# Linear attention and an fp8 product on one core: V's product moved ahead of the inter product, the fp8 and output products behind the intra product, and the output read one step later

## The chip, the cores and the metric

The kernel runs on one core of a Trainium2 chip. A core has TensorE (matmuls), VectorE, ScalarE and GpSimd (elementwise work and reductions) and SyncE, whose queue here starts most of the DMAs. Each engine executes its own instructions in program order and waits on semaphores for the others. The metric is device time in microseconds (us), lower is better; the kernel before takes 1250.56 us (median of 3 runs, 1250.27 to 1251.45).

## The reference, cut to what matters

```python
xn = layernorm(x)                                # x: (4, 2048, 512)
q, k, v = (heads(xn @ W.T + b) for W, b in ...)  # 64 heads of 8
q, k = softmax(be * q), softmax(be * k)          # over the 8 values of a head, be = exp(beta)
kv = cumsum(einsum('zsD,zsd->zsDd', k, v), axis=1)
kn = cumsum(k, axis=1)
att = einsum('zsD,zsDd->zsd', q, kv) / sum(q * kn, axis=-1)
ffn = fp8(clip(xn / s_in, -448, 448)) * s_in @ (w_fp8 * s_w).T + bias
out = x + (att @ Wo.T + bo) + ffn                # att with its heads joined again
```

## The kernel before, in words

The sequence is cut into 64 steps of 32 positions; with four sequences a tile has 128 rows, and a step handles one such tile of x (128 x 512). Prefix sums are done in chunks: within a step, scores of q and k are masked to the lower triangle and multiplied with v (the "intra product", L1018); what came before the step is in a running state, and q times this state is the "inter product" (L999). Both add up in the PSUM tile `a_ps`, in which the step's own state update (k times v, `state()`, L917) stands before; VectorE must have read that (`mask_state`, L654) before L999 may overwrite it.

Products of fp32 accuracy are made from pairs of fp16 matmuls. Projecting K, Q or V (`project()`, L873 to L877) is 12 matmuls of 128x128x512, the output product (`project_out()`, L884 to L888) 12 more, and the fp8 product (L975) 4. V's projection, the fp8 product and the output product use the same PSUM tile `vo_ps`. For step i it is filled in turn by: V's projection of i; VectorE's `scale_values(i)` (L727) reads it and writes `vp`; ScalarE copies the output bias into it (the seed, L477, signalled by `oseed_ready`); the fp8 product and then the output product of step i-2 add to it; VectorE's `output()` (L720) reads it, adds the residual and writes `o_sb`.

The four compute engines each have a function `body(i)`, and it alone sets the order on its engine. The engines are joined by counting semaphores. In program order one `body(i)` issues, with t = i-1:

- TensorE: K(i); scores of t, first half, and state update; transposes of the normalised attention of i-2; Q(i); scores and state, second half; fp8(i-2); output product(i-2); inter product(t); V(i); intra product(t).
- VectorE: normalise attention(i-2) (L682, L690); xn(i+1) (L618); fp8 clip (L637); row maximum and shift of K (L643, L647), which needs K(i); two masks of scores (L671); first `mask_state`; low part of the attention (L748); key sums and the transpose of k (L699 to L711); maximum and shift of Q; fp8 rounding constants (L624, L629); two masks; the transpose `qT` (L769), which needs ScalarE's exponential of Q; second `mask_state`; `output(i-2)`; `add_state` (L665); statistics of x; `scale_values(i)`.
- ScalarE: the seed for step i-2; copies of xn; exponential of K; seed of K; high part of the attention; `k_pairs`; exponential of Q; seed of Q; `q_heads(i)`, four masked copies of `qT` (L521); `st_seqs`, four masked copies of the running state (L530).
- SyncE's queue: moves of `vp` into `v_groups` (8 DMAs, step i-1); turned copies of x; loads of x; the store of out(i-2); the load of the residual.

Steps 0 to 3 and 60 on are written out; between them the compute engines other than TensorE loop over groups of four steps. TensorE has all steps written out for weights whose low fp16 part is zero in the fp8 product, as here.

Of the kernel before, what the change touches and what calls it, by code (L numbers as in the profile page):

```python
# [28 lines left out]
ACT = mybir.ActivationFunctionType  # L29
# [3 lines left out]
SEQS = 4  # L33
TOK = P // SEQS
# [4 lines left out]
J = 4  # L39
GP = 2  # L40
SP = 2
# [81 lines left out]
def build(nc, x, wq, bq, wk, bk, wv, bv, wo, bo, beta, wf, bf, in_scale, w_scale, const, out):  # L123
# [3 lines left out]
    with ExitStack() as ctx:  # L127
# [173 lines left out]
        def _(sp):  # L301
# [29 lines left out]
            def body(i):  # L331
                if (i - 1).exists():
                    move_v(i - 1)
                if (i + 1).exists():
                    turn_x(i + 1)
                if i.exists():
                    turn_xq(i)
                if (i + SLOTS).exists():
                    load_x(i + SLOTS)
                t = i - 2  # L340
                if t.exists():
                    sp.wait_ge(o_ready, (t + 1).n)
                    sp.dma_start(out_t[t.n], o_sb[:, t.parity, :]).then_inc(stored[t.parity], 16)
                if i.exists():
                    sp.dma_start(x_res[:, i.parity, :], x_t[i.n]).then_inc(r_loaded[i.parity], 16)
# [14 lines left out]
            for i in range(STEPS + 2):  # L360
                body(Step(0, i))
# [89 lines left out]
        def _(act):  # L451
# [16 lines left out]
            def body(i, last_weights=None, fold=False):  # L468
                t = i - 2
                if t.exists():  # L470
                    if (t + 1).exists():
                        act.wait_ge(vp_ready, (t + 2).n)
                    else:
                        act.wait_ge(o_ready, t.n)
                    if t.off == 0 and isinstance(t.k, int):
                        act.wait_ge(fold_ready, 1)
                    sc.activation(vo_ps[:, :], bias[:, 3, :], ACT.Copy, scale=out_up[:, :])\  # L477
                        .then_inc(oseed_ready, 1)
# [22 lines left out]
                if i.exists():  # L501
# [21 lines left out]
                    last.then_inc(qheads_ready, 1)  # L523
                t = i - 1
# [51 lines left out]
        def _(dve):  # L576
# [154 lines left out]
            def body(i, last_weights=None, fold=False):  # L731
# [5 lines left out]
                if i.exists():  # L737
                    if i.after(1):
                        quantise(i)
                    shift(i, k_ps, k_done, k_max, kmax_ready, k_shift, kshift_ready, ke_ready)  # L740
# [121 lines left out]
        def _(pe):  # L862
# [58 lines left out]
            def body(i, low_part=True, last_weights=None, fold=False):  # L921
# [42 lines left out]
                if fold:  # L964
# [4 lines left out]
                    project_out(rest=False).then_inc(bvo_done, 1)  # L969
                t = i - 2  # L970
# [15 lines left out]
                t = i - 1  # L986
                if t.exists():
                    pe.wait_ge(qT_ready, (t + 1).n)
                    if i.exists():
                        pe.wait_ge(masked_ready, (t + 1).n * 2)  # L990
                    else:
                        pe.wait_ge(an_ready, t.n)
                    if t.after(1):
                        pe.wait_ge(stseqs_ready, t.n)
                    for n in range(2):
                        for gp in range(GP):
                            for u in range(J):
                                g = G // 2 * n + GP * u + gp
                                mm(a_rows[TOK * u:TOK * (u + 1), n, gp, :], qT[:, t.parity, g, :],  # L999
                                   st_seqs[:, t.parity, g].rearrange("p j b w -> p (j b w)"),  # L1000
                                   start=(gp == 0), stop=False, skip_group_check=True)
                if i.exists():
                    if fold:
                        pe.wait_ge(fold_ready, 1)
                    if (i - 2).exists():
                        pe.wait_ge(o_ready, (i - 1).n)
                    project(vo_ps, i, MV, seeded=False).then_inc(v_done, 1)
                if t.exists():
                    pe.wait_ge(att_ready, (t + 1).n * 4)
                    for b in range(SEQS):  # L1010
                        pe.wait_ge(v_moved[t.parity][b], (t + 2).half * 16 * GP)
                    pe.sem_inc(pe_waited, 1)
                    for h in range(2):
                        for n in range(SEQS // SP):
                            for j in range(J):
                                cols = slice(GW * j + SP * VW * n, GW * j + SP * VW * (n + 1))
                                for u in range(J):
                                    last = mm(a_rows[TOK * u:TOK * (u + 1), h, :, cols],  # L1018
                                              att[:, n, J * h + u, j, :],
                                              v_groups[:, t.parity, :, n, J * h + u, j, :], start=False, stop=True,  # L1020
                                              skip_group_check=True)
                    last.then_inc(a_done, 1)
# [71 lines left out]
```

## Time and profile before

| | kernel before |
|---|---|
| median of 3 runs | 1250.56 us |
| profiled execution | 1250.03 us |
| its span, first to last instruction | 1248.2 us |
| mean granted TensorE clock over the span | 0.982 of full |
| TensorE matmuls, busy | 1174.9 us (94%) |
| VectorE, busy | 977.9 us (78%) |
| ScalarE, busy | 744.9 us (60%) |
| GpSimd, busy | 321.6 us (26%) |
| DMA, mean of the core | 84 GB/s |

The profiled execution stands beside the runs: 1250.03 against 1250.56 us. A page of the profile gives shares over the whole span; the question of a change in order is answered by views in time order, where each row is an instruction (or a run of equal ones) with its start, its length and, in brackets, the idle time of its engine before it and who ended it. Matmuls are pipelined: a row's length of 0.38 us holds the pipeline's depth, and what a matmul costs in a dense run is the distance to the next start, 0.22 us.

### The profile page before, as it was taken

The page shows a single profiled execution, that of the slowest core. Times are in us where ns is not written, and L with a number is a line of the kernel's source. Part 1 is how long each engine was busy: PE and PEld are TensorE (multiplying, and loading weights), DVE is VectorE, ACT ScalarE, POOL GpSimd, SP SyncE. Part 2 cuts the span into 40 slices and gives each one's busy share as a digit, 9 for nine tenths or more (in the row PEclk, how much of TensorE's full clock was granted, in tenths as well). Part 3 has the DMA queues.
Part 4 walks back from the last instruction along what each step waited for, and adds up shares of the span by engine and source line. Part 5 has one row for each costly group of instructions (what it writes and reads, how often), then busy time and mean ns, then how long its engine had stood idle before and what let it go on. Part 6 is the DMA issues. An engine that isn't in the chain of part 4 may idle for free.

```text
span 1248.2 us, 60447 instructions
## 1 busy us (share of the span) xinstructions
PE 1174.9 (94%) x26082; PEld 679.2 (54%) x26082; DVE 977.9 (78%) x1968; ACT 744.9 (60%) x1177; POOL 321.6 (26%) x590
## 2 busy tenths in 40 slices
PE   1459999999999999999999999999999999999996
PEld 1235555555555555555555555555555555555553
DVE  4567887888788788878878887788788778878873
ACT  0456656665666666566666656666665666566652
POOL 3122222322222232222223232222323232222310
PEclk9689999999999999999999999999999999999999
DMA  9022334334334433433333343343343433333331
GB/s 234 21 59 70 81 90 89 78 80 91 82 82 87 89 80 79 90 86 80 85 89 82 77 90 89 78 84 91 81 79 91 84 83 81 91 82 81 72 73 46
DMA packets 156483, 104.64 MB, mean 84 GB/s; under 512 B 111968, under 2 KB 128480, under 8 KB 156256
## 3 DMA queue, kind: packets, MB, share of 16 engines
q1 hardware_dynamic: 155536, 99.76, 35.7%
q8 instruction: 209, 3.42, 1.2%
q10 hardware_dynamic: 720, 1.31, 0.4%
q14 instruction: 18, 0.15, 0.0%
HBM read 40.20 MB, written 16.78 MB: 46 GB/s over the span
## 4 chain that ended last, share of the span: by engine, by line
PE 92%; issue 3%; DVE 2%; DMA 1%; ACT 1%; POOL 1%; SPq 0%; POOLq 0%; DVEq 0%; ACTq 0%
PE s_ps L900 10%; PE a_ps L917 7%; PE a_ps L1018 6%; PE a_ps L999 6%; PE k_ps L873 5%; PE vo_ps L975 5%; PE vo_ps L873 5%; PE k_ps L877 5%; PE k_ps L875 5%; PE vo_ps L884 4%; PE vo_ps L888 4%; PE vo_ps L886 4%; PE vo_ps L877 4%; PE vo_ps L875 4%; PE q_ps L877 4%; PE q_ps L873 4%
## 5 line engine op out<-in xcount | busy, mean ns | idle before, releaser
L521 ACT ACTIVATE q_heads<-qT,cst 128x512 f32<-128x512 f32 x256 | 163.9, 711 | 88.2 <-DVE qT L769 88.2
L407 POOL TENSOR_TENSOR y_sum<-y,y_magic 128x512 f32<-128x512 f32 x64 | 81.4, 1272 | 433.0 <-DVE y_magic L629 433.0
L506 ACT ACTIVATE w_own<-kT,cst 128x512 f32<-128x512 f32 x128 | 85.5, 715 | 166.7 <-DVE kT L711 166.7
L530 ACT ACTIVATE st_seqs<-st_run,cst 128x576 f32<-128x576 f32 x252 | 181.5, 797 | 0.5 <-DVE st_run L665 0.5
L671 DVE TENSOR_TENSOR att<-s_ps,cst 128x512 f32<-128x512 f32 x256 | 163.8, 682 | 0.4 <-PE s_ps L900 0.4
L400 POOL TENSOR_TENSOR x_split<-xn,x_split 128x512 f16<-128x512 f32 x64 | 74.1, 1158 | 291.6 <-ACT x_split L462 284.3
L900 PE MATMUL s_ps<-q_heads,w_own 64*64 64x128 f32 x4096 | 141.3, 275 | 0.6 <-DVE att L671 0.6
L900 PEld LDWEIGHTS s_ps<-q_heads,w_own 64*64 64x64 f32 x4096 | 110.4, 132 | 54.3 <-issue 54.2
L462 ACT ACTIVATE x_split<-xn 128x512 f16<-128x512 f32 x64 | 40.3, 630 | 126.7 <-DVE xn L618 126.7
L873 PE MATMUL k_ps<-w_hi,xT 128*128 128x512 f16 x256 | 98.9, 386 | 17.0 <-DMA xT<-x_split 12.3
L727 DVE TENSOR_TENSOR vp<-vo_ps,vp 128x512 f32<-128x512 f32 x64 | 44.3, 692 | 86.3 <-PE vo_ps L877 86.3
L884 PE MATMUL vo_ps<-w_hi,ah 128*128 128x512 f16 x260 | 98.5, 379 | 0.6 <-DVE al L748 0.6
L888 PE MATMUL vo_ps<-w_hi,al 128*128 128x512 f16 x260 | 98.5, 379 | 0.0
L886 PE MATMUL vo_ps<-w_lo,ah 128*128 128x512 f16 x260 | 98.5, 379 | 0.0
L875 PE MATMUL k_ps<-w_lo,xT 128*128 128x512 f16 x256 | 98.3, 384 | 0.0
L877 PE MATMUL k_ps<-w_hi,xT 128*128 128x512 f16 x256 | 98.3, 384 | 0.0
L873 PE MATMUL vo_ps<-w_hi,xT 128*128 128x512 f16 x256 | 97.7, 382 | 0.0
L917 PE MATMUL a_ps<-vp,k_e 32*32 32x36 f32 x8064 | 97.6, 196 | 0.0
L873 PE MATMUL q_ps<-w_hi,xT 128*128 128x512 f16 x256 | 97.0, 379 | 0.0
L875 PE MATMUL q_ps<-w_lo,xT 128*128 128x512 f16 x256 | 97.0, 379 | 0.0
L877 PE MATMUL q_ps<-w_hi,xT 128*128 128x512 f16 x256 | 97.0, 379 | 0.0
L875 PE MATMUL vo_ps<-w_lo,xT 128*128 128x512 f16 x256 | 97.0, 379 | 0.0
(136 smaller groups left out, 2287.8 us busy)
## 6 DMA issues: line engine op xcount, KB each, us to landing
v_groups<-vp SPq DMA_DIRECT2D x512, 36.0 KB, 3.1
x_in<-L_attn_x SPq DMA_DIRECT2D x64, 256.0 KB
x_res<-L_attn_x SPq DMA_DIRECT2D x64, 256.0 KB
out<-o_sb SPq DMA_DIRECT2D x64, 256.0 KB
w_own<-L_attn_Wk SPq DMA_DIRECT2D x1, 1024.0 KB, 13.0
w_own<-L_attn_Wq SPq DMA_DIRECT2D x1, 1024.0 KB, 15.0
w_own<-L_attn_Wv SPq DMA_DIRECT2D x1, 1024.0 KB, 16.5
att<-L_ffn_weight_fp SPq DMA_DIRECT2D x1, 1024.0 KB, 18.1
```

The costliest lines, as they stand in the source:

```text
L506: last = sc.activation(k_pairs[:, i.parity, :, c, :], kT[:, :, :], ACT.Copy, scale=pair_mask[:, c:c + 1])
L521: last = sc.activation(q_heads[:, i.parity, :, j, :], qT[:, i.parity, :, :], ACT.Copy, scale=head_mask[:, j:j + 1])
L530: last = sc.activation(st_seqs[:, i.parity, :, :, b, :].rearrange("p g j w -> p (g j) w"), st_run[:, :, :, :].rearrange("p g j w -> p (g j ...
L671: v.tensor_tensor(att[:, c % 2, 4 * (c // 2):4 * (c // 2) + 4, :, :] .rearrange("p g j s -> p (g j) s"), s_ps[:, DM * (c % 2):DM * (c % 2 ...
L873: mm(bank[:, :], xT[:, t.parity, 0, c, :], w_hi[:, m, c, :], start=(c == 0 and not seeded), stop=False, skip_group_check=seeded)
L875: mm(bank[:, :], xT[:, t.parity, 0, c, :], w_lo[:, m, c, :], start=False, stop=False, skip_group_check=seeded)
L877: last = mm(bank[:, :], xT[:, t.parity, 1, c, :], w_hi[:, m, c, :], start=False, stop=(c == KC - 1), skip_group_check=seeded)
L884: mm(vo_ps[:, :], ah[:, j, :], w_hi[:, MO, j, :], start=(j == 0 and not rest), stop=False, skip_group_check=rest)
L886: mm(vo_ps[:, :], ah[:, j, :], w_lo[:, MO, j, :], start=False, stop=False, skip_group_check=rest)
L888: last = mm(vo_ps[:, :], al[:, j, :], w_hi[:, MO, j, :], start=False, stop=(j == J - 1), skip_group_check=rest)
L900: last = mm(s_ps[SP * TOK * gp:SP * TOK * (gp + 1), DM * n + P * q:DM * n + P * (q + 1)], k_pairs[rows, t.parity, g, :, :].rearrange("p c ...
L917: last = mm(a_ps[rows, col:col + J * VW], k_e[rows, t.parity, TOK * g:TOK * (g + 1)], vp[rows, t.parity, v_head(g):v_head(g) + J, :], star ...
```

## The change

On TensorE, `body(i)` ends in another order: V(i), inter product(t), intra product(t), fp8(i-2), output product(i-2), where before it was fp8, output, inter, V, intra. ScalarE's seed for i-2 moves from the start of `body(i+1)` to `body(i)`, behind `q_heads(i)` and ahead of `st_seqs`. VectorE's `output()` moves from behind the second `mask_state` of `body(i)` to the next body, ahead of K's maximum; `scale_values(i)` comes directly behind `add_state`, and the statistics behind it. On SyncE's queue the moves of v(i) stand last in the body, and the store goes one step later. No instruction is added or removed. With two lines more in the file, line numbers differ: L999 becomes L991, L1018 becomes L1004, L975 becomes L1014, L477 becomes L522, L769 becomes L771.

The end of a step on TensorE before, from the last three matmuls of the output product on (`ah`, `al`: attention, high and low part; `st_seqs`: the running state):

```order
L884 MATMUL vo_ps<-w_hi,ah 128x512
L886 MATMUL vo_ps<-w_lo,ah 128x512
L888 MATMUL vo_ps<-w_hi,al 128x512
L999 MATMUL a_ps<-st_seqs,qT 32x144 [waits stseqs_ready,masked_ready,qT_ready]
L999 MATMUL a_ps<-st_seqs,qT 32x144 x15
L873 MATMUL vo_ps<-w_hi,xT 128x512 [waits o_ready]
L875 MATMUL vo_ps<-w_lo,xT 128x512
L877 MATMUL vo_ps<-w_hi,xT 128x512
```

And now the same place, from the last of V's matmuls on:

```order
L877 MATMUL vo_ps<-w_lo,xT 128x512
L879 MATMUL vo_ps<-w_hi,xT 128x512
L991 MATMUL a_ps<-st_seqs,qT 32x144 [waits stseqs_ready,masked_ready,qT_ready]
L991 MATMUL a_ps<-st_seqs,qT 32x144 x15
L1004 MATMUL a_ps<-v_groups,att 32x2x18 [waits v_moved0_2,v_moved0_3,v_moved0_1,att_ready,v_moved0_0]
L1004 MATMUL a_ps<-v_groups,att 32x2x18 x63
L1014 MATMUL vo_ps<-w_hi,xq 128x512 [waits oseed_ready,xq_turned]
L1014 MATMUL vo_ps<-w_hi,xq 128x512 x3
L886 MATMUL vo_ps<-w_hi,ah 128x512 [waits al_ready,ah_ready]
```

V's projection is what now stands between the second state update and the inter product, where the fp8 and the output product stood; the inter and the intra product are neighbours, and they alone stand between V and the fp8 product, which waits on `oseed_ready`.

ScalarE in the same step, before:

```order
L512 ACTIVATE q_e<-q_shift,q_exp_scale 128x512 [waits qT_ready,qshift_ready]
L515 ACTIVATE q_ps<-bias 128x512
L521 ACTIVATE q_heads<-qT,cst 128x16x32 [waits scores_done,qT_ready]
L521 ACTIVATE q_heads<-qT,cst 128x16x32 x3
L530 ACTIVATE st_seqs<-st_run,cst 128x64x9 [waits a_done,strun_ready]
L530 ACTIVATE st_seqs<-st_run,cst 128x64x9 x3
L477 ACTIVATE vo_ps<-bias,out_up 128x512 [waits vp_ready]
L459 REGISTER_ALU
```

ScalarE now:

```order
L502 ACTIVATE q_e<-q_shift,q_exp_scale 128x512 [waits qT_ready,qshift_ready]
L505 ACTIVATE q_ps<-bias 128x512
L511 ACTIVATE q_heads<-qT,cst 128x16x32 [waits scores_done,qT_ready]
L511 ACTIVATE q_heads<-qT,cst 128x16x32 x3
L522 ACTIVATE vo_ps<-bias,out_up 128x512 [waits vp_ready]
L530 ACTIVATE st_seqs<-st_run,cst 128x64x9 [waits a_done,strun_ready]
L530 ACTIVATE st_seqs<-st_run,cst 128x64x9 x3
L459 REGISTER_ALU
```

The seed (`vo_ps<-bias,out_up`) has gone ahead of the four `st_seqs` copies, and still stands behind the four `q_heads` copies.

VectorE from the second pair of score masks on, before:

```order
L671 TENSOR_TENSOR att<-s_ps,cst 128x512 [waits scores_done] x2
L769 STREAM_TRANSPOSE qT<-q_e 128x512 [waits a_done,qheads_ready,qe_ready]
L654 TENSOR_TENSOR st_masked<-a_ps,cst 128x288 [waits state_done]
L720 SCALAR_TENSOR_TENSOR o_sb<-vo_ps,out_dn,x_res 128x512 [waits stored0,r_loaded0,o_done]
L662 REGISTER_ALU
L665 TENSOR_TENSOR st_run<-st_run,st_masked 128x576 [waits stseqs_ready,masked_ready]
L592 BN_STATS stats<-x_in 128x6 [waits x_loaded1]
```

VectorE now:

```order
L671 TENSOR_TENSOR att<-s_ps,cst 128x512 [waits scores_done] x2
L771 STREAM_TRANSPOSE qT<-q_e 128x512 [waits a_done,qheads_ready,qe_ready]
L654 TENSOR_TENSOR st_masked<-a_ps,cst 128x288 [waits state_done]
L662 REGISTER_ALU
L665 TENSOR_TENSOR st_run<-st_run,st_masked 128x576 [waits stseqs_ready,masked_ready]
L727 TENSOR_TENSOR vp<-vo_ps,vp 128x64x8 [waits krec_ready,v_done]
L592 BN_STATS stats<-x_in 128x6 [waits x_loaded1]
```

The read of the output has left this place; what stands ahead of the second `mask_state` (L654) is unchanged.

The diff, without the parts that only repeat moved lines:

```diff
@@ SyncE, body(i)
-                if (i - 1).exists():
-                    move_v(i - 1)
                 if (i + 1).exists():
                     turn_x(i + 1)
                 if i.exists():
                     turn_xq(i)
                 if (i + SLOTS).exists():
                     load_x(i + SLOTS)
-                t = i - 2
+                t = i - 3
                 if t.exists():
                     sp.wait_ge(o_ready, (t + 1).n)
                     sp.dma_start(out_t[t.n], o_sb[:, t.parity, :]).then_inc(stored[t.parity], 16)
+                if (i - 1).exists():
+                    sp.dma_start(x_res[:, (i - 1).parity, :], x_t[(i - 1).n]).then_inc(r_loaded[(i - 1).parity], 16)
                 if i.exists():
-                    sp.dma_start(x_res[:, i.parity, :], x_t[i.n]).then_inc(r_loaded[i.parity], 16)
+                    move_v(i)
@@ ScalarE, body(i): taken from its start, put behind q_heads
+                t = i - 2
+                if t.exists():
+                    if i.exists():
+                        act.wait_ge(vp_ready, (i + 1).n)
+                    else:
+                        act.wait_ge(o_ready, t.n)
+                    if t.off == 0 and isinstance(t.k, int):
+                        act.wait_ge(fold_ready, 1)
+                    sc.activation(vo_ps[:, :], bias[:, 3, :], ACT.Copy, scale=out_up[:, :])\
+                        .then_inc(oseed_ready, 1)
@@ VectorE, body(i)
                     if i.after(1):
                         quantise(i)
+                    if (i - 3).exists():
+                        output(i - 3)
                     shift(i, k_ps, k_done, k_max, kmax_ready, k_shift, kshift_ready, ke_ready)
...
-                if (i - 2).exists():
-                    output(i - 2)
                 if t.exists() and i.exists():
                     add_state(t)
+                if i.exists():
+                    scale_values(i)
                 if (i + 3).exists():
                     statistics(i + 3)
                 if i.parity == 0 and (i + PAIR).exists():
                     variances(i + PAIR)
-                if i.exists():
-                    scale_values(i)
+                if not (i + 1).exists() and (i - 2).exists():
+                    output(i - 2)
@@ TensorE, body(i): V, taken from behind the inter product
+                if i.exists():
+                    if fold:
+                        pe.wait_ge(fold_ready, 1)
+                    if (i - 3).exists():
+                        pe.wait_ge(o_ready, (i - 2).n)
+                    project(vo_ps, i, MV, seeded=False).then_inc(v_done, 1)
                 t = i - 1
                 if t.exists():
                     pe.wait_ge(qT_ready, (t + 1).n)
...
                     last.then_inc(a_done, 1)
+                t = i - 2
+                if t.exists():
+                    pe.wait_ge(xq_turned, (t + 1).n * 16)
+                    pe.wait_ge(oseed_ready, (t + 1).n)
...
+                    last.then_inc(f_done, 1)
+                t = i - 2
+                if t.exists():
+                    pe.wait_ge(ah_ready, (t + 1).n)
+                    pe.wait_ge(al_ready, (t + 1).n)
+                    project_out(rest=True).then_inc(o_done, 1)
```

## Rows read from the trace of the kernel before

**Rows 1.** The page: busy shares, and TensorE's busy share and clock in 40 slices.

```profile
PE 1174.9 (94%) x26082; PEld 679.2 (54%) x26082; DVE 977.9 (78%) x1968; ACT 744.9 (60%) x1177; POOL 321.6 (26%) x590
...
PE   1459999999999999999999999999999999999996
...
PEclk9689999999999999999999999999999999999999
```

**Rows 2.** The chain that ended last, by engine (page, part 4).

```profile
PE 92%; issue 3%; DVE 2%; DMA 1%; ACT 1%; POOL 1%; SPq 0%; POOLq 0%; DVEq 0%; ACTq 0%
```

**Rows 3.** TensorE in time order: start us, us, engine, line, shapes, count, [idle before].

```profile
616.96 0.84 PE L917 MATMUL a_ps<-vp,k_e 32*32 32x36 f32 x64
617.73 1.04 PE L975 MATMUL vo_ps<-w_hi,xq 128*128 128x512 f16 x4
...
620.98 0.38 PE L888 MATMUL vo_ps<-w_hi,al 128*128 128x512 f16 x1
621.53 1.19 PE L999 MATMUL a_ps<-st_seqs,qT 128*32 128x144 f32 x32 [0.17 <-issue]
622.65 0.39 PE L873 MATMUL vo_ps<-w_hi,xT 128*128 128x512 f16 x1
...
625.34 1.32 PE L1018 MATMUL a_ps<-v_groups,att 128*32 128x36 f32 x128
626.60 0.39 PE L873 MATMUL k_ps<-w_hi,xT 128*128 128x512 f16 x1
...
628.98 0.38 PE L877 MATMUL k_ps<-w_hi,xT 128*128 128x512 f16 x1
```

**Rows 4.** VectorE in time order, same columns: an even step.

```profile
611.13 0.69 DVE L643 TENSOR_REDUCE k_max<-k_ps 128x64 f32<-128x512 f32 x1 [0.56 <-PE k_ps L877]
...
619.18 1.28 DVE L671 TENSOR_TENSOR att<-s_ps,cst 128x512 f32<-128x512 f32 x2
620.38 0.70 DVE L769 STREAM_TRANSPOSE qT<-q_e 128x512 f32<-128x512 f32 x1
621.01 0.42 DVE L654 TENSOR_TENSOR st_masked<-a_ps,cst 128x288 f32<-128x288 f32 x1
...
622.06 0.75 DVE L665 TENSOR_TENSOR st_run<-st_run,st_masked 128x576 f32<-128x576 f32 x1
...
629.40 0.69 DVE L643 TENSOR_REDUCE k_max<-k_ps 128x64 f32<-128x512 f32 x1 [0.55 <-PE k_ps L877]
```

**Rows 5.** VectorE: an odd step.

```profile
593.10 0.69 DVE L643 TENSOR_REDUCE k_max<-k_ps 128x64 f32<-128x512 f32 x1 [0.55 <-PE k_ps L877]
...
602.10 0.70 DVE L769 STREAM_TRANSPOSE qT<-q_e 128x512 f32<-128x512 f32 x1
```

**Rows 6.** VectorE: first regular step, then the last key product.

```profile
121.22 0.69 DVE L643 TENSOR_REDUCE k_max<-k_ps 128x64 f32<-128x512 f32 x1 [0.55 <-PE k_ps L877]
...
130.07 0.70 DVE L769 STREAM_TRANSPOSE qT<-q_e 128x512 f32<-128x512 f32 x1
...
1209.64 0.69 DVE L643 TENSOR_REDUCE k_max<-k_ps 128x64 f32<-128x512 f32 x1 [1.00 <-PE k_ps L877]
```

**Rows 7.** ScalarE in time order, the even step.

```profile
621.12 2.56 ACT L521 ACTIVATE q_heads<-qT,cst 128x512 f32<-128x512 f32 x4 [1.40 <-DVE qT L769]
623.59 2.88 ACT L530 ACTIVATE st_seqs<-st_run,cst 128x576 f32<-128x576 f32 x4
626.36 0.66 ACT L477 ACTIVATE vo_ps<-bias,out_up 128x512 f32<-128x512 f32 x1
```

**Rows 8.** TensorE in the last steps.

```profile
1232.18 1.19 PE L999 MATMUL a_ps<-st_seqs,qT 128*32 128x144 f32 x32
1233.18 1.47 PE L1018 MATMUL a_ps<-v_groups,att 128*32 128x36 f32 x128
```

**Rows 9.** VectorE, the last output read.

```profile
1241.05 0.75 DVE L720 SCALAR_TENSOR_TENSOR o_sb<-vo_ps,out_dn,x_res 128x512 f32<-128x512 f32 x1 [2.94 <-PE vo_ps L888]
```

**Rows 10.** The last stretch: us, busy us of each engine (x), PEclk, DMA share, GB/s.

```profile
1224.00:1241.00 17.00, 13.88 (x360) 8.64 (x350) 7.60 (x16) 2.73 (x5) 0.00 (x0) 1.00 0.23 65
```

More of the change, by code:

```diff
@@ L359, in _ @@
             sp.wait_ge(v_cleared, 2)
-            for i in range(STEPS + 2):
+            for i in range(STEPS + 3):
                 body(Step(0, i))
@@ L468, in body @@
             def body(i, last_weights=None, fold=False):
[L469 to L478, printed above, removed]
                 if (i + 1).exists():
@@ L969, in body @@
                     project_out(rest=False).then_inc(bvo_done, 1)
+                if i.exists():
[4 more added lines that the diff above has]
+                    project(vo_ps, i, MV, seeded=False).then_inc(v_done, 1)
+                t = i - 1
+                if t.exists():
+                    pe.wait_ge(qT_ready, (t + 1).n)
+                    if i.exists():
+                        pe.wait_ge(masked_ready, (t + 1).n * 2)
+                    else:
+                        pe.wait_ge(an_ready, t.n)
+                    if t.after(1):
+                        pe.wait_ge(stseqs_ready, t.n)
+                    for n in range(2):
+                        for gp in range(GP):
+                            for u in range(J):
+                                g = G // 2 * n + GP * u + gp
+                                mm(a_rows[TOK * u:TOK * (u + 1), n, gp, :], qT[:, t.parity, g, :],
+                                   st_seqs[:, t.parity, g].rearrange("p j b w -> p (j b w)"),
+                                   start=(gp == 0), stop=False, skip_group_check=True)
+                if t.exists():
+                    pe.wait_ge(att_ready, (t + 1).n * 4)
+                    for b in range(SEQS):
+                        pe.wait_ge(v_moved[t.parity][b], (t + 2).half * 16 * GP)
+                    pe.sem_inc(pe_waited, 1)
+                    for h in range(2):
+                        for n in range(SEQS // SP):
+                            for j in range(J):
+                                cols = slice(GW * j + SP * VW * n, GW * j + SP * VW * (n + 1))
+                                for u in range(J):
+                                    last = mm(a_rows[TOK * u:TOK * (u + 1), h, :, cols],
+                                              att[:, n, J * h + u, j, :],
+                                              v_groups[:, t.parity, :, n, J * h + u, j, :], start=False, stop=True,
+                                              skip_group_check=True)
+                    last.then_inc(a_done, 1)
                 t = i - 2
@@ L985, in body @@
                     project_out(rest=True).then_inc(o_done, 1)
[L986 to L1022, printed above, removed]
             def transpose_weights(m):
```

## The prediction, made before the changed kernel was run

> **What bounds the kernel now.** I read the page first, then the chain of waits, then time-ordered views of a few steps, engine by engine. The page says that TensorE is busy in 94% of the span and, outside the first and the last slices, 9 tenths or more everywhere, at the full granted clock; VectorE is at 78%, ScalarE at 60% [rows 1]. The chain that ended last is TensorE for 92% [rows 2]. By that alone the kernel is TensorE's, and a new order of the same matmuls could only win or lose small change. The steps say more. From one reading of K's product by VectorE (`k_max`) to the next there are 18.27 us in the step at 611.13 [rows 4]. Over the 60 regular steps from 121.22 to 1209.64 the mean is 1088.42 / 60 = 18.14 us [rows 6]. In the even step the inter product (L999) starts at 621.53, while the last output matmul before it started at 620.98 [rows 3]: a gap of 0.55 where neighbours in a dense run are 0.22 apart, and 0.17 of it is marked idle. What ended at that moment is VectorE's second `mask_state`: 621.01 + 0.42 = 621.43 [rows 4], 0.10 before L999 starts. L999 must wait for it, since it overwrites what the mask reads. So VectorE is only just hidden. It is late although its inputs are there: the state update begins at 616.96, so the scores were done by then [rows 3], and VectorE comes to mask them at 619.18 [rows 4], 2.2 us later. From `k_max` on VectorE runs one queue of work, and reaches the end of `qT` 9.95 us (621.08) and the end of the mask 10.30 us after `k_max` began [rows 4]. In the odd step `qT` ends 602.80 - 593.10 = 9.70 after it [rows 5], in the steps written out at both ends 130.77 - 121.22 = 9.55 [rows 6]. TensorE and VectorE are thus two nearly equal bounds, and what counts is how much TensorE work is queued between K's product and the first matmul that needs the end of that VectorE queue.
>
> **The change, part by part.** I count from the start of `k_max` (0), in the even step.
>
> No matmul is added or removed: the sum on TensorE itself is the old 18.1 us or slightly less. The order between inter and intra product can be seen in the last steps, where they are already neighbours: L1018 starts 1.00 after L999 and lasts 1.47 [rows 8], so the pair takes 2.47; before, L999 to V's first matmul takes 1.12 and L1018 to K's first 1.26 [rows 3], 2.38 together. Bounds for what the new neighbours save or cost: -0.1 to +0.1 us a step. I take 0, since it will not be on the path.
>
> Inter product. The matmul that used to start the fp8 product starts at 617.73 - 611.13 = +6.60 [rows 3, 4]. V's 12 matmuls stand there now, 12 x 0.216 = 2.6 and 0.1 for the change to small tiles, where fp8 and output product gave 16 x 0.216 + 0.1 = 3.6. TensorE comes to L999 at +9.3, but the mask ends at +10.30 and nothing ahead of it on VectorE has changed (`output` stood behind it). L999 starts at +10.40: a wait of about 1.1 (0.8 in odd steps), and inter and intra product end their issue at about +12.9.
>
> The seed. Before, it started at 626.36 for an fp8 product many microseconds later [rows 7]. Now it must come after `scale_values` of the same step. VectorE: mask end +10.30, `add_state` 0.75 [rows 4], `scale_values` some 0.7 as the other 128x512 operations, so +11.7. V's product is long there by then. ScalarE, however, is in order and has the four `q_heads` copies ahead of the seed. They start at 621.12, 0.04 after `qT`, which is +9.99, and the next instruction starts at 623.59, +12.46 [rows 7]. So the seed starts at +12.46, ends 0.66 later at +13.12 [rows 7], and with 0.12 for the signal (0.10 at L999 above) the fp8 product starts at +13.24. That is 0.3 after TensorE is through with the intra product: a second wait, and the one that sets the period.
>
> Behind it fp8, output and K stand in one dense run: first fp8 to last output matmul 620.98 - 617.73 = 3.25, one more distance 0.22, first to last matmul of K 628.98 - 626.60 = 2.38, and from there to `k_max` 629.40 - 628.98 = 0.42 [rows 3, 4]: 6.26 in all. The new period is 13.24 + 6.26 = 19.50 in an even step; 9.70 for 9.95 gives 19.25 in an odd one, and 9.55 gives 19.10 outside the loop. K's product can't be read earlier, and VectorE's queue can't start before it, so the loop of waits closes: K, VectorE until `qT`, `q_heads`, seed, fp8, output, K.
>
> Parts with no price, and their cover. `output` moved ahead of `k_max`: the output product ends some 2.7 before K's does, and the read takes 0.75 [rows 9], so it fits into VectorE's wait. Statistics and variances behind `scale_values` (about 1.5) run while TensorE does intra, fp8 and output product. `st_seqs`, 2.88 on ScalarE [rows 7], ends near +16.0, the copies of xn near +17.3, and the next exponential of K is wanted near +20.9. V's moves start earlier against their reader: `vp` is ready at +11.7, and its readers come after the next `k_max`. On SyncE's queue the turned copy of x passes behind the same eight moves as before and has a whole step. If one of these covers failed, the price would be its own size, 0.5 to 0.8 a step.
>
> Ends. In step 2 the same lengthening, 1.0. In step 1 V now stands behind VectorE's fold of the bias, with the inter product no longer in front to cover it: about 0.7 (an operation like `output`). At the end, VectorE is in order and must take `output(61)` and `output(62)` ahead of the normalisations that the last transposes wait for. I followed the last steps with the same durations: from the last `k_max` to the end of the last output read, 1241.80 - 1209.64 = 32.16 before [rows 6, 9] and about 33.9 now, +1.7.
>
> The sum: 56 loop steps at 19.375 (mean of 19.50 and 19.25) and 4 at 19.10 are 1161.4, less 1088.42 = +73.0; start +1.7, end +1.7. Together +76.4. The profiled execution took 1250.03 us (span 1248.2), so its like is 1326.4; the runs' median lies 0.5 above it, 1250.56, and so the forecast is 1327 us, 6.1% slower.
>
> The clock. In the last 17 us TensorE is busy for 13.88 only, so it idles for 3.12 in several pieces, and the granted clock stays 1.00, the 2.4 GHz level [rows 10]. The new waits, 1.4 of 19.4 us, are a smaller share, and I leave the clock as it is. The Trainium skill (TensorE: Matmul & The Clock Gate, "A second HAM failure mode: psum-queue depth-cycling") speaks against this: a kernel whose TensorE idles briefly and often between groups of matmuls had its clock fall and rise again. No stretch of this trace bears that out. By that rule parts of the dense run behind each wait would go at 1.2 GHz, and it is a rival below.
>
> **The rivals.**
>
> A. The seed is hidden, only L999 waits: if ScalarE were free for it, or took `q_heads` faster. Then fp8 follows the intra product: +10.40 + 1.00 + 1.26, and up to 0.16 for the longer L1018, is +12.8, the period 19.08 in even and 18.8 in odd steps. +0.8 a step, with the ends 1302. Against it: `q_heads` was timed with nothing else in its way [rows 7].
>
> B. Faster: VectorE's queue gives way. If the queue from `k_max` to the mask took under 9.3 instead of 10.30 and `q_heads` and seed slid under the intra product, TensorE would set the period. It would win the 0.17 idle of the even steps and up to 0.1 at the joints: 18.14 - 0.13 = 18.0, 1242 us. The decisive point is the 9.3. For it, only the gap between `k_max` and what was queued; against it, nothing is removed from that queue, and its operations keep their sizes.
>
> C. A further cover fails, for instance `output` ahead of `k_max` or SyncE's queue: 0.5 to 0.8 a step more, 1357 to 1375.
>
> D. The clock falls in the run behind each wait. Its 28 matmuls at half speed would cost 28 x 0.216 = 6.0 a step; if only one step in ten, +38, 1365.
>
> E. The change doesn't do what it says: the two waits sit as before because the mask or the seed isn't what TensorE waits for; then no change, 1250.
>
> **How the numbers follow.** Forecast 0.80, A 0.08, B 0.04, C 0.04, D 0.03, E 0.01. A change can be told from none here at 0.2%, about 2.5 us. The forecast's own error is some 0.1 us a step from the signal times and the joints, +-6, and 0.15 more if the difference between even and odd steps (0.25) takes one side: 1312 to 1336. The range goes a little toward A and C: 1308 to 1338. Slower holds all but B and E: 0.95; same 0.01; faster 0.04.
>
> **What would show it.** `k_max` every 19.4 us or so. On TensorE two waits in each step: ahead of the inter product, some 0.8 to 1.1 us, ended by `st_masked`, and ahead of the first fp8 matmul, 0.2 to 0.4, ended by ScalarE's `vo_ps`. On ScalarE the seed right behind `q_heads`, with no idle time. VectorE's idle time ahead of `k_max` should grow, and `output` should wait for the output product. TensorE's busy share should fall to about 90%. A period of 19.0 with no wait ahead of the fp8 product is A; a period of 18.0 is B; a PEclk below full in the middle slices is D. The forecast is wrong if `qT` ends much earlier than 9.7 after `k_max`.

## The result: 10% slower, more than forecast

The changed kernel takes 1381.18 us (median of 4 runs, 1373.33 to 1390.28) against 1250.99 for the kernel before, a ratio of 1.104 with a 95% interval of 1.097 to 1.112. Forecast were 1327 us (1308 to 1338) and slower. The runs of the changed kernel lie 17 us apart, those of before 1.2.

The page of the changed kernel, as [rows 1] and [rows 2] of before:

```profile
PE 1179.0 (86%) x26082; PEld 693.9 (50%) x26082; DVE 1004.0 (73%) x1968; ACT 745.2 (54%) x1177; POOL 322.1 (23%) x590
...
PE   1569989898998989889889998988898899899895
...
PEclk8789999999999999999999999999999999999997
...
PE 35%; DVE 27%; issue 21%; ACT 13%; DMA 1%; DVEq 1%; POOL 0%; ACTq 0%; SPq 0%; POOLq 0%
```

TensorE's busy time is the same (1179.0 for 1174.9 us) in a longer span (1377.0 us, the profiled execution 1378.77). The chain that ended last is no longer TensorE's: VectorE has 27%, ScalarE 13%, and 21% is "issue", time in which the engine waited for nothing that the profile shows. It was 3%.

A step without disturbance, TensorE first (start us, us, engine, line, tile, count, [idle before]), the rows that answer to [rows 3]:

```profile
650.77 0.76 PE L919 MATMUL a_ps<-vp,k_e 32*32 32x36 f32 x64
...
655.08 1.19 PE L991 MATMUL a_ps<-st_seqs,qT 128*32 128x144 f32 x32 [0.85 <-DVE qT L771]
656.06 1.31 PE L1004 MATMUL a_ps<-v_groups,att 128*32 128x36 f32 x128
657.96 1.02 PE L1014 MATMUL vo_ps<-w_hi,xq 128*128 128x512 f16 x4 [0.59 <-ACT vo_ps L522]
```

VectorE and ScalarE in the same step, as [rows 4, 7]:

```profile
644.95 0.69 DVE L643 TENSOR_REDUCE k_max<-k_ps 128x64 f32<-128x512 f32 x1 [0.89 <-PE k_ps L879]
...
653.94 0.70 DVE L771 STREAM_TRANSPOSE qT<-q_e 128x512 f32<-128x512 f32 x1
654.56 0.42 DVE L654 TENSOR_TENSOR st_masked<-a_ps,cst 128x288 f32<-128x288 f32 x1
655.02 1.19 DVE L665 TENSOR_TENSOR st_run<-st_run,st_masked 128x576 f32<-128x576 f32 x1
...
664.20 0.69 DVE L643 TENSOR_REDUCE k_max<-k_ps 128x64 f32<-128x512 f32 x1 [1.84 <-PE k_ps L879]
```

```profile
654.67 2.57 ACT L511 ACTIVATE q_heads<-qT,cst 128x512 f32<-128x512 f32 x4 [1.40 <-DVE qT L771]
657.14 0.67 ACT L522 ACTIVATE vo_ps<-bias,out_up 128x512 f32<-128x512 f32 x1
```

`k_max` to `k_max` is 19.25 us. TensorE waits 0.85 ahead of the inter product. The bracket names `qT`, but `qT` ended at 654.64; what ended just before L991 starts at 655.08 is `mask_state`'s `st_masked`, at 654.98. It waits 0.59 ahead of the fp8 product for the seed, which ScalarE starts when the `q_heads` copies are done. Over the regular steps undisturbed periods are 19.25 and 19.53 in turn inside the loop and 19.12 outside; forecast were 19.25, 19.50 and 19.10.

The next step is of another kind:

```profile
674.60 1.19 PE L991 MATMUL a_ps<-st_seqs,qT 128*32 128x144 f32 x32 [1.12 <-DVE qT L771]
675.58 1.10 PE L1004 MATMUL a_ps<-v_groups,att 128*32 128x36 f32 x104
678.23 0.40 PE L1004 MATMUL a_ps<-v_groups,att 128*32 128x36 f32 x24 [1.54 <-issue]
678.56 1.04 PE L1014 MATMUL vo_ps<-w_hi,xq 128*128 128x512 f16 x4
```

104 matmul records into the intra product TensorE stands still for 1.54 us, marked "issue", with no wait on a semaphore anywhere near: the 128 records are one run of matmuls behind one set of waits. This period is 20.62. There are 25 such stops over 0.3 us in the regular steps, 44.1 us together; the kernel before has none over 0.3.

In some steps a third thing follows. TensorE's fp8 and output product after a wait of 0.59 and a stop of 1.27 close together:

```profile
154.52 0.38 PE L1014 MATMUL vo_ps<-w_hi,xq 128*128 128x512 f16 x1 [0.59 <-ACT vo_ps L522]
156.17 0.82 PE L1014 MATMUL vo_ps<-w_hi,xq 128*128 128x512 f16 x3 [1.27 <-issue]
...
157.67 0.63 PE L886 MATMUL vo_ps<-w_hi,ah 128*128 128x512 f16 x1
158.10 0.63 PE L888 MATMUL vo_ps<-w_lo,ah 128*128 128x512 f16 x1
...
160.66 0.40 PE L888 MATMUL vo_ps<-w_lo,ah 128*128 128x512 f16 x1
160.89 0.38 PE L890 MATMUL vo_ps<-w_hi,al 128*128 128x512 f16 x1
```

From 157.67 to 160.66 neighbouring starts are 0.43 apart, not 0.22: the 1.2 GHz level.

### The profile page after: what moved, and what is told of

It is laid out like the page before. It is cut to its first block, busy times and chain, and to the rows that moved or that the text cites. A ratio compares the mean times of both kernels' runs of the same rounds, so it can differ in the third digit from the quotient of the medians.

```text
span 1377.0 us, 60448 instructions
## 1 busy us (share of the span) xinstructions
PE 1179.0 (86%) x26082; PEld 693.9 (50%) x26082; DVE 1004.0 (73%) x1968; ACT 745.2 (54%) x1177; POOL 322.1 (23%) x590
## 3 DMA queue, kind: packets, MB, share of 16 engines
q8 instruction: 209, 3.42, 1.1%
q10 hardware_dynamic: 720, 1.31, 0.3%
HBM read 40.20 MB, written 16.78 MB: 41 GB/s over the span
## 4 chain that ended last, share of the span: by engine, by line
PE 35%; DVE 27%; issue 21%; ACT 13%; DMA 1%; DVEq 1%; POOL 0%; ACTq 0%; SPq 0%; POOLq 0%
ACT q_heads L511 6%; PE vo_ps L1014 5%; PE vo_ps L886 4%; PE vo_ps L888 4%; PE vo_ps L890 4%; PE k_ps L879 4%; PE k_ps L875 4%; PE k_ps L877 4%; DVE att L671 4%; DVE k_max L643 3%; DVE k_shift L647 3%; DVE k_sum L699 3%; DVE kT L711 3%; DVE qT L771 3%; DVE q_max L643 3%
## 5 line engine op out<-in xcount | busy, mean ns | idle before, releaser
L476 ACT ACTIVATE k_e<-k_shift,k_exp_scale 128x512 f32<-128x512 f32 x64 | 46.3, 723 | 224.8 <-DVE k_shift L647 224.8
L991 PE MATMUL a_ps<-st_seqs,qT 128*32 128x144 f32 x2048 | 76.2, 288 | 58.0 <-DVE qT L771 58.0
L1004 PE MATMUL a_ps<-v_groups,att 128*32 128x36 f32 x8192 | 88.8, 198 | 40.6 <-issue 40.2
L643 DVE TENSOR_REDUCE k_max<-k_ps 128x64 f32<-128x512 f32 x64 | 44.3, 692 | 96.7 <-PE k_ps L879 96.7
L720 DVE SCALAR_TENSOR_TENSOR o_sb<-vo_ps,out_dn,x_res 128x512 f32<-128x512 f32 x64 | 47.9, 748 | 83.6 <-PE vo_ps L890 83.3
L1004 PEld LDWEIGHTS a_ps<-v_groups,att 128*32 128x32 f32 x8192 | 86.4, 108 | 43.4 <-issue 43.4
L991 PEld LDWEIGHTS a_ps<-st_seqs,qT 128*32 128x32 f32 x2048 | 59.0, 109 | 87.5 <-DVE qT L771 86.3
L886 PE MATMUL vo_ps<-w_hi,ah 128*128 128x512 f16 x260 | 102.6, 395 | 0.0
L888 PE MATMUL vo_ps<-w_lo,ah 128*128 128x512 f16 x260 | 102.1, 393 | 0.3 <-issue 0.3
L890 PE MATMUL vo_ps<-w_hi,al 128*128 128x512 f16 x260 | 102.0, 392 | 0.0
```

The lines of the kernel that those rows point to most:

```text
L886: mm(vo_ps[:, :], ah[:, j, :], w_hi[:, MO, j, :], start=(j == 0 and not rest), stop=False, skip_group_check=rest)
L888: mm(vo_ps[:, :], ah[:, j, :], w_lo[:, MO, j, :], start=False, stop=False, skip_group_check=rest)
L890: last = mm(vo_ps[:, :], al[:, j, :], w_hi[:, MO, j, :], start=False, stop=(j == J - 1), skip_group_check=rest)
L1004: last = mm(a_rows[TOK * u:TOK * (u + 1), h, :, cols], att[:, n, J * h + u, j, :], v_groups[:, t.parity, :, n, J * h + u, j, :], start=Fal ...
```

## Where the 128.7 us are

Between the two profiled executions (1378.77 - 1250.03 = 128.7) the time splits at the `k_max` marks. Up to the first regular one: 122.10 against 121.22, +0.9. The 60 regular steps: 1203.57 against 1088.42, +115.2. From the last `k_max` to the last output read: 44.92 against 32.16, +12.8. If all 60 steps were undisturbed they would take 28 x 19.53 + 28 x 19.25 + 4 x 19.12 = 1162.3, +73.9; the other 41.3 us come from the stops and the clock. The stops sum to 44.1, but where one falls it mostly swallows the 0.59 wait that follows: some 14 us less, leaves 30. Four steps have eight dense matmul distances each of 0.43 instead of 0.216, 6.6 us together; the granted clock is full in all the other 56. The last 4 us are about 0.15 more behind each stop than its idle time, which I have not placed.

## The experiments

Theory when they were planned: the two waits are as forecast, and the stops come from TensorE's supply of instructions, which run out because two products of many small matmuls now follow each other. Rival: the stops are a wait for data or a semaphore that the profile doesn't name, an echo of the new waits. Ratios are to the kernel before, run on the same chip.

**Seed ahead of q_heads.** ScalarE of the changed kernel, order in `body(i)`:

```diff
-  q_heads(i); seed(i - 2); st_seqs
+  seed(i - 2); q_heads(i); st_seqs
```

> The changed kernel with ScalarE's seed of the output product put ahead of the four q_heads copies instead of behind them. In the changed kernel's trace the steps without an idle stretch in the middle of the intra product last 19.25 and 19.54 us, and there TensorE waits 0.59 us ahead of the fp8 product. Theory (the period is VectorE's queue until qT, then q_heads, then seed, then fp8, output, K): the seed is then ready 0.4 us or more before the intra product ends, the wait ahead of the fp8 product vanishes, the wait ahead of the inter product (0.85 and 1.13) stays, and clean steps shorten by about 0.5 us to 18.8 and 19.1. Rival (the seed is not what the fp8 product waits for, it is late for another reason): clean steps stay at 19.25 and 19.54. The idle stretches in the middle of the intra product, which hit about 26 steps, should stay in both, and each costs more now since no wait absorbs a part: about 1350 us in all, against 1381.

Measured: 1368.85 us, ratio 1.097 (1.094 to 1.099), where about 1350 was expected; by the medians alone it can't be told from the changed kernel's 1.104 (1.097 to 1.112), by the steps it can. Undisturbed periods are 18.97 and 19.26, 0.28 less each, not 0.5. A step of it, all engines:

```profile
610.88 1.19 DVE L666 TENSOR_TENSOR st_run<-st_run,st_masked 128x576 f32<-128x576 f32 x1
612.00 0.68 DVE L728 TENSOR_TENSOR vp<-vo_ps,vp 128x512 f32<-128x512 f32 x1
```

```profile
612.71 0.69 ACT L515 ACTIVATE vo_ps<-bias,out_up 128x512 f32<-128x512 f32 x1 [3.57 <-DVE vp L728]
613.34 2.54 ACT L522 ACTIVATE q_heads<-qT,cst 128x512 f32<-128x512 f32 x4
```

```profile
613.55 1.02 PE L1015 MATMUL vo_ps<-w_hi,xq 128*128 128x512 f16 x4 [0.31 <-ACT vo_ps L515]
```

The fp8 product did wait for the seed, which waited for `q_heads`: shown. With that gone the seed waits for V's scaling, and this is late because `add_state` takes 1.19 us here, not the 0.75 of [rows 4]. So a wait of 0.31 is left.

**Second mask_state early.** VectorE of the changed kernel:

```diff
+                if t.exists() and i.exists():
+                    mask_state(t, 1)
                 if t.exists():
                     mask_scores(t, 2)
                     mask_scores(t, 3)
...
-                if t.exists() and i.exists():
-                    mask_state(t, 1)
```

> The changed kernel with VectorE's second read of the state (mask_state) put ahead of the second pair of score masks and of the transpose qT. Theory: the wait ahead of the inter product (0.85 and 1.13 us) vanishes, yet the kernel gets slower, since qT now ends 0.38 us later and with it q_heads, the seed and the fp8 product: clean steps 19.63 and 19.92, the wait ahead of the fp8 product grows from 0.59 to about 1.9. Together with the idle stretches in the intra product, which now are partly hidden by that wait, 1380 to 1400 us. Rival (the wait ahead of the inter product is itself a cost that adds up): clean steps shorten to 18.3 to 18.5, and the kernel to about 1320.

Measured: 1388.69 us, 1.110 (1.108 to 1.112). The changed kernel's own runs reach from 1373 to 1390 us, so the medians don't tell the two apart; the steps do. The wait ahead of the inter product is gone, and undisturbed periods are 19.62 and 19.90, 0.37 longer: the wait of 0.85 to 1.13 us cost nothing, since the loop closes over `qT`, `q_heads` and the seed. I had not expected the third kind of period, 21.57:

```profile
393.42 1.19 PE L991 MATMUL a_ps<-st_seqs,qT 128*32 128x144 f32 x32
394.43 1.29 PE L1004 MATMUL a_ps<-v_groups,att 128*32 128x36 f32 x128
397.87 1.36 PE L1014 MATMUL vo_ps<-w_hi,xq 128*128 128x512 f16 x4 [2.15 <-ACT vo_ps L522]
399.02 0.63 PE L886 MATMUL vo_ps<-w_hi,ah 128*128 128x512 f16 x1
399.44 0.63 PE L888 MATMUL vo_ps<-w_lo,ah 128*128 128x512 f16 x1
...
401.93 0.38 PE L888 MATMUL vo_ps<-w_lo,ah 128*128 128x512 f16 x1
402.14 0.38 PE L890 MATMUL vo_ps<-w_hi,al 128*128 128x512 f16 x1
```

```profile
396.00:399.00 3.00, 1.13 (x4) 0.47 (x5) 2.74 (x11) 3.00 (x5) 0.68 (x4) 0.90 0.22 69
399.00:402.00 3.00, 3.00 (x9) 1.14 (x8) 0.85 (x3) 1.53 (x4) 1.67 (x9) 0.53 0.21 56
402.00:405.80 3.80, 3.80 (x22) 1.60 (x24) 0.97 (x3) 1.24 (x2) 1.16 (x1) 1.00 0.22 47
```

(Columns: stretch, us, busy us of each engine, granted clock, DMA share, GB/s.) Behind this wait of 2.15 us the granted clock is 0.90, 0.53 and 1.00 in three successive stretches, and eight or nine matmuls stand 0.43 us apart: 1.7 us a step, in 21 of the 60 steps. So rival D of the prediction is real, at 1.7 us and not 6.0 a step. The Trainium skill's rule that I weighed there (TensorE: Matmul & The Clock Gate, "A second HAM failure mode: psum-queue depth-cycling") agrees with these rows.

Which steps are hit doesn't follow from the length of one pause. Two other steps of this run, the first a wait of 2.15 as well, the second without any wait of TensorE, but with a stop of 1.79:

```profile
238.14 1.02 PE L1014 MATMUL vo_ps<-w_hi,xq 128*128 128x512 f16 x4 [2.15 <-ACT vo_ps L522]
847.60 0.33 PE L1004 MATMUL a_ps<-v_groups,att 128*32 128x36 f32 x12 [1.79 <-issue]
```

```profile
224.48:244.38 19.90, 17.75 (x412) 10.52 (x416) 15.46 (x32) 11.46 (x18) 6.06 (x15) 1.00 0.27 71
834.40:855.97 21.57, 19.67 (x412) 11.06 (x416) 15.57 (x33) 11.42 (x18) 6.09 (x15) 0.92 0.28 73
```

The first kept the full clock (its step is 224.48 to 244.38), the second did not (834.40 to 855.97). Of the 21 steps 15 had a wait of 2.13 to 2.44 us and 6 no wait above 0.97 and no stop above 1.79; four waits of 2.15 or 2.16 were followed by full speed.

**Both, and V scaled ahead of qT.** No engine's queue should then hold TensorE up. The new order, in words:

```text
   ScalarE:  seed(i - 2); q_heads(i); st_seqs
   VectorE:  magic(i + 1); mask_state(t, 1); mask_scores(t, 2); mask_scores(t, 3);
             scale_values(i); qT; add_state(t); statistics
```

> The changed kernel with both edits (seed ahead of q_heads, second mask_state ahead of the second pair of score masks) and with V's scaling ahead of the transpose qT. By the durations of the trace no engine then waits for VectorE or ScalarE in a step: clean steps 18.0 us, as TensorE's own work. What is left over 1251 is then the price of the idle stretches alone. Theory A, they come from TensorE's supply of instructions (they recur at the same place modulo 256 instructions, whatever TensorE waited for before): they stay, some 24 of 1.5 to 2.4 us, and the time is 1275 to 1310. Theory B, they are a late echo of the waits ahead of the inter and fp8 products (a data or semaphore wait that the profile names badly): they vanish, and the time is 1238 to 1248.

Measured: 1275.37 us, 1.020 (1.019 to 1.022). No wait for another engine is left on TensorE in the regular steps, undisturbed periods are 17.7 to 18.0, and the stops are there, 22 over 0.3 us, 22.8 us together. Theory A: the waits are not their cause. They may lengthen them: in this run and the one before, which both lack the wait ahead of the inter product, a stop has 1.0 us in the mean, in the changed kernel 44.1 / 25 = 1.8. But a run further down has neither wait and 1.5, so this is not shown.

**The kernel before, second mask_state early.** The same edit as above on the kernel before.

> The kernel before with one edit: VectorE's second mask_state ahead of the second pair of score masks and of qT. In its trace, odd periods are 18.0 and even ones 18.28 us, and the 0.28 was put down to VectorE's second mask_state, which ends 0.10 us before the inter product starts. Theory: all periods become 18.0, and the kernel takes 8 us less: 1243, ratio 0.993 to 0.995. Rival (the 0.28 is TensorE's own, the mask only happens to end there): no change, 1251.

Measured: 1240.31 us (5 runs), 0.9925 (0.991 to 0.994). The regular steps take 1078.69 us, 17.98 each, and there is no stop over 0.3 us. This is the fastest kernel of the study: the old order on TensorE with VectorE's late read of the state moved. Expected were 1243 and 0.993 to 0.995. It confirms the reading of [rows 3, 4] that VectorE set the start of the inter product in every other step.

**The kernel before with inter and intra product as neighbours.** TensorE's `body(i)`; VectorE's `scale_values` goes into the next body with it:

```diff
-  fp8(i-2); output product(i-2); inter(t); V(i); intra(t)
+  fp8(i-2); output product(i-2); inter(t); intra(t); V(i)
```

> The kernel before with its fp8 and output products where they were, but V's projection moved behind the intra product, so that inter and intra product are neighbours as in the changed kernel; VectorE scales V after the fp8 clip of the next step. Nothing waits for the seed or for V here. Theory A (supply of instructions: the small matmuls of inter and intra product, 160 matmul records and as many weight loads in some 2.5 us, follow each other without a dense product between them): idle stretches of 1.5 to 2.4 us appear in the middle of the intra product in about one step of three, as in the changed kernel, which did not have one before; 1275 to 1310 us. Theory B (they come from the changed kernel's waits or from V's moves being issued while the intra product runs): none appear, the time is 1245 to 1258.

Measured: 1309.27 us, 1.048 (1.046 to 1.051). Stops appear, 26 over 0.3 us with 38.6 us, mostly inside the intra product, and none of the changed kernel's waits is there:

```profile
642.76 1.19 PE L1000 MATMUL a_ps<-st_seqs,qT 128*32 128x144 f32 x32 [0.25 <-issue]
643.73 1.42 PE L1013 MATMUL a_ps<-v_groups,att 128*32 128x36 f32 x99
646.64 0.46 PE L1013 MATMUL a_ps<-v_groups,att 128*32 128x36 f32 x29 [1.49 <-issue]
```

So the neighbourhood, with V's product no longer between the two, is enough to make them; the changed kernel's waits, its earlier seed and its later read of the output are not needed. The step had another cost too, which I had not foreseen: undisturbed periods are 18.2 and 18.5, against 18.0 and 18.28 before, and the intra product there takes up to 1.80 us. That part is not explained.

**Three instructions more in a step.** TensorE of the changed kernel:

```diff
                     project_out(rest=True).then_inc(o_done, 1)
+                if i.exists():
+                    for _ in range(3):
+                        pe.sem_inc(pe_waited, 1)
```

> The changed kernel with three semaphore increments more in each step of TensorE. In the changed kernel the idle stretch inside the intra product moves by 6 matmul records every 4 steps (99, 105, 111, 117, 123 records into it) and 5 steps take it back by 25, which fits 829 instructions a step and blocks of 256. Theory A: with 832 = 3.25 x 256 instructions a step the idle stretch stands at the same record in every fourth step, all through the kernel, where there is one. Theory B (a wait for data): the place goes on wandering or has no rule. Time within 1360 to 1400 in both.

Measured: 1378.99 us, 1.103 (1.099 to 1.106). The intra product in four steps:

```profile
686.49 1.31 PE L1004 MATMUL a_ps<-v_groups,att 128*32 128x36 f32 x128
...
705.75 1.31 PE L1004 MATMUL a_ps<-v_groups,att 128*32 128x36 f32 x128
...
725.29 1.26 PE L1004 MATMUL a_ps<-v_groups,att 128*32 128x36 f32 x123
728.70 0.26 PE L1004 MATMUL a_ps<-v_groups,att 128*32 128x36 f32 x5 [2.15 <-issue]
...
747.95 0.99 PE L1004 MATMUL a_ps<-v_groups,att 128*32 128x36 f32 x91
751.15 0.54 PE L1004 MATMUL a_ps<-v_groups,att 128*32 128x36 f32 x37 [2.21 <-issue]
```

The stops no longer wander. From step 4 to step 60 every fourth step has one after record 123, the step behind it one after record 91 (all 30 at exactly these counts), and the other two steps have none. 123 - 91 = 32 records with as many weight loads are 64 instructions, which is 832 - 3 x 256. A wait for data can't know this. It is the border of a block of 256 instructions that TensorE stops at.

The trace of the changed kernel says the same by itself. Number TensorE's records (matmuls, weight loads, semaphore instructions) in order of time: all 25 stops of the regular steps fall on place 193 or 194 of a count by 256. So do all 26 of the run before this one.

**No loads of x and of the residual.** This kernel leaves out the loads of x from step 4 and of the residual from step 2 on, and with them VectorE's waits for these loads; the tiles of the first steps are used again:

```diff
-                if (i + SLOTS).exists():
-                    load_x(i + SLOTS)
...
-                if (i - 1).exists():
+                if (i - 1).exists() and i.off <= 2:
                     sp.dma_start(x_res...
...
```

> The changed kernel without the loads of x and of the residual after the first steps (x_in of steps 4 on and x_res of steps 2 on are left out, 128 KB or more a step less traffic; the first tiles are used again). Theory A1 (the block of instructions takes some 2 us to come by itself, other traffic does not matter): idle stretches as before, 1370 to 1385. Theory A2 (the instruction blocks are late because they queue behind the big loads on the same DMA engines): idle stretches vanish or shrink by more than half, and the time falls to 1328 to 1350.

Measured: 1389.05 us, 1.111 (1.108 to 1.113). Loads gone, stops as before: 28 of them, 50.3 us, at the same records (99, 105, 111, 117, 123 in steps 5, 9, 13, 17, 21). What was read from HBM fell from 40.20 to 8.22 MB, so the blocks are not late because of these loads; whether the moves of V or the turned copies of x matter was not tried. The expected range was 1370 to 1385. The two runs, 1387 and 1391 us, lie at the upper end of the changed kernel's, with more stops and more steps at the low clock (8 against 4); no cause is claimed for that.

**TensorE's steps in a loop.** `iterations(pe, ...)` for the written-out steps:

```diff
-                for i in range(2, STEPS + 2):
-                    body(Step(0, i), low_part=False)
+                iterations(pe, lambda i: body(i, low_part=False), first=2)
```

> The changed kernel with TensorE's steps 4 to 59 as a loop of four steps, as the other engines have them, instead of written out. Theory A: the code of an iteration is the same each time and begins at the same address, so the idle stretches stand at the same record of the same step of the four in every iteration, and one more short stop comes at each jump back (in the kernel before a jump cost 0.85 us): 1360 to 1410. Theory B (data or semaphores): no relation to the iteration.

Measured: 1370.48 us, 1.096 (1.094 to 1.098). In every iteration the intra product stops once, in its first step, after record 126, for 1.45 to 2.47 us, and the jump back costs 0.4 to 0.9 us ahead of K, as expected. In 9 of the 14 iterations the scores of the first step also start 0.3 to 0.6 us late, which was not expected.

## Why the prediction was wrong

What held: the two bounds, both waits, their places and releasers, and the period, to 0.03 us in each of its three kinds. The fp8 product's wait is 0.59 where 0.2 to 0.4 was forecast, because inter and intra product take 2.29 us in a row (655.08 to 657.37) and not 2.47; as the seed sets the period, that cost nothing. The undisturbed step accounts for +73.9 us where +73.0 was forecast. That the inter product's wait is free and the seed's is not is shown by the two edits that take up one each. The start (+1.7 forecast, +0.9) was near enough.

What failed first is the step on the inter and intra product as neighbours: "bounds for what the new neighbours save or cost: -0.1 to +0.1 us a step. I take 0, since it will not be on the path". I priced it from the one place where they had been neighbours, [rows 8], and a single pair says nothing of a cost that falls in two steps of five. The term is 34.7 us net in the regular steps (41.3 less 6.6 for the clock), 0.6 a step. I had counted the matmuls of a stretch by their time alone, never by their number. Inter and intra product are 160 matmul records and as many weight loads, 320 instructions in 2.4 us, where the dense products need 24 instructions for 2.6 us. The profile has the supply on record:

```profile
q8 instruction: 1, 0.02, 64.6%
```

(DMA queue, kind: packets, MB, share of 16 engines, from 675.9 to 676.0.) One packet of the instruction queue, 1.0 us of one engine by its share (64.6% of 16 x 0.1), starts at 675.99; TensorE, standing since 676.69, goes on at 678.23. So it is at every stop: in all 25 TensorE goes on 2.2 to 2.7 us after such a packet started, and in 24 of them it had started less than 1.5 us before TensorE stood still. The page counts 209 of them with 3.42 MB, 16 KB each, as does the page of the kernel before, which has no such stop. At 829 instructions a step TensorE crosses a border 3.24 times a step, and in 24 of the 25 stops the border falls into the last part of the intra product (record 67 and later) or at the fp8 product's start. My reading, which no run tests by itself: there the block before has been used up fastest. With V's product between the two, as in the kernel before, the same borders cost nothing over 0.3 us. What triggers the load of a block, and so how long it has, the runs don't show; all but one of the stops are 1.0 to 2.4 us long. That they vary from run to run, as the times do, is likely but was not measured.

The Trainium skill has this mechanism (Runtime: NRT & Kernel Launch, "Instruction fetch mechanics"): the sequencer refills in 16 KiB blocks of 256 instructions over its own DMA queue, and the cost of a border is said to be mostly hidden. The block size agrees with the packets here and with the three added instructions; "mostly hidden" held before the change and not behind it.

The second step that failed: "I leave the clock as it is". The argument was that the new waits are a smaller share of a step than 3.12 us of idle time in 17, which went by at full clock [rows 10]. The stops add to them, and the clock fell in 4 of the 60 regular steps, 6.6 us, and again at the end. TensorE's waits and stops sum to 2.84 to 3.04 us in those four steps, but to as much as 3.25 in others that kept the full clock: neither one pause nor their sum tells which step is hit, and that stays open. The trace before also had the clock low in slices of its start [rows 1], which I passed over. I gave rival D 3%, one step in ten and 6.0 us a step. It came in one step of fifteen at 1.65 us. It is no case of its own but a part of the result. Of the other rivals, A and C didn't come; B's numbers, 18.0 us a step and 1242 us, are reached by the kernel before with `mask_state` moved (17.98 and 1240), another change than the one B was about.

The third is the end, +1.7 forecast, +12.8 measured. By the changed kernel's trace two stops (1.91 and 2.53 us) fall there, and both last fp8 and output products run at the low clock but for their last two or three matmuls, 27 distances of 0.43, 5.6 us more than at full clock. That makes 10 of the 11.1 us that the forecast lacks:

```profile
1350.00:1355.00 5.00, 2.47 (x38) 1.06 (x25) 0.00 (x0) 0.00 (x0) 0.00 (x0) 0.69 0.16 57
1355.00:1360.00 5.00, 4.34 (x12) 1.33 (x10) 0.62 (x1) 0.00 (x0) 0.00 (x0) 0.62 0.00 0
```

The range's upper end had 0.25 us a step at most for errors of the working, and nothing for a resource that the sum didn't have.

## What to carry to other kernels

Where TensorE's program is written out, ask of a new order how many instructions, weight loads included, follow each other without a dense product between: small fp32 matmuls in long rows emptied the instruction supply here, and V's product of 12 matmuls of 512 columns between two such rows hid it. When a wait is seen on an engine, follow the loop that closes over it before removing it; here removing the longer wait made the undisturbed step 0.37 us longer. And when two engines are nearly equal bounds, look for an operation that can be read early at no cost: one moved read of the state gave 0.75% on the kernel before.

## What the runs showed of the hardware

TensorE's instructions come in blocks of 256, as 16 KB packets of a DMA queue; in the changed kernel every stop at a border ended 2.2 to 2.7 us after the start of a packet. After pauses of 1 to 2.4 us in otherwise dense steps the granted clock fell in some steps to the 1.2 GHz level for eight or nine dense matmuls (397.87 to 401.93 above), and after equal pauses in others it did not. And VectorE's `add_state`, whose operands all lie in SBUF, takes 0.71 to 0.76 us when GpSimd is idle or within 0.1 us of the end of its rounding, and 1.18 to 1.31 when it starts some 0.6 us before that end:

```profile
654.32 1.28 POOL L411 TENSOR_TENSOR y_round<-y_sum,y_magic 128x512 f32<-128x512 f32 x1
```

In the changed kernel this runs until 655.60 and `add_state` from 655.02 to 656.21; in the last step, where there is no rounding, it took 0.76. The score masks, which read PSUM, take 1.28 a pair in both kernels, beside GpSimd or not. This is an observation over the kernels of this study, not an experiment of its own; it cost the changed kernel nothing, as the seed waited for `q_heads`, and 0.3 us a step once it didn't.
